# Moving Y's evictions between the statistics, and X's border issues from SP to ACT, in a two-block convolution stack

## The reference

```python
x = x + _L0_conv_ref(_gn(x), w1, w3, w5, alpha)
x = x + _L1_conv_ref(_gn(x), w, b)
```

## Time and profile before

| what | us |
|---|---|
| median of three runs | 420.05 |
| lowest and highest run | 417.27, 420.19 |
| the profiled execution | 415.32 |
| its span on the core | 413.5 |
| busy in it: PE, DVE, ACT, POOL | 318.6, 318.4, 304.0, 261.8 |

### The profile page before, as it was taken

The page is one execution under the profiler, slowest core; times in us unless marked ns, Lnnn a source line. Parts: engine busy times, 40 slices in busy tenths (PEclk is TensorE's granted clock), DMA queues, the critical chain, the costliest instruction groups (busy, mean ns, idle before and its releaser), DMA issues.

```text
span 413.5 us, 12579 instructions
## 1 busy us (share of the span) xinstructions
PE 318.6 (77%) x5206; PEld 281.8 (68%) x5206; DVE 318.4 (77%) x688; ACT 304.0 (74%) x372; POOL 261.8 (63%) x206
## 2 busy tenths in 40 slices
PE   2494849727979797979797879879897979897530
PEld 2363637616969797967696769777896779796320
DVE  7776989854778989877888696969797777599520
ACT  1317734199969999979797996989796989957320
POOL 6414525077867888768778585868585878855511
PEclk9997797995989999989898998999898999999675
DMA  7569496201996669666976789767976527701955
GB/s 154 156 193 243 122 239 140 74 6 51 201 214 182 190 186 220 169 181 195 228 192 173 197 211 220 196 192 178 219 181 191 161 61 198 201 20 48 272 165 152
DMA packets 113213, 70.01 MB, mean 169 GB/s; under 512 B 4732, under 2 KB 110084, under 8 KB 113156
## 3 DMA queue, kind: packets, MB, share of 16 engines
q1 hardware_dynamic: 106464, 65.90, 62.7%
q10 hardware_dynamic: 6692, 3.30, 3.2%
HBM read 41.10 MB, written 28.09 MB: 167 GB/s over the span
## 4 chain that ended last, share of the span: by engine, by line
DVE 46%; PE 18%; SPq 12%; DMA 10%; ACT 4%; issue 4%; ACTq 2%; POOLq 0%; POOL 0%; DVEq 0%
DVE xt L698 25%; PE ps L378 17%; DVE stats L642 17%; DMA haloX<-edge_scratch 3%; DMA xt<-in_x_dram 3%; SPq L264 3%; SPq L238 3%; ACT gn_f L552 2%; SPq L304 1%; DMA edge_scratch<-gnY 1%; ACTq L245 1%; SPq L245 1%; DMA edge_scratch<-gnX 1%; SPq L251 1%; ACT cross L562 1%
## 5 line engine op out<-in xcount | busy, mean ns | idle before, releaser
L378 PE MATMUL ps<-gnX,band 64*64 64x512 f16 x2880 | 192.4, 414 | 44.4 <-DVE xt L698 32.6
L378 PEld LDWEIGHTS ps<-gnX,band 64*64 64x64 f16 x2880 | 168.5, 189 | 61.4 <-issue 54.4
L698 DVE SCALAR_TENSOR_TENSOR xt<-ps,unscale,xt 128x512 f32<-128x512 f32 (+1 forms) x194 | 143.6, 747 | 40.1 <-PE ps L378 37.7
L868 POOL TENSOR_TENSOR gnX<-gn_f,gnX 128x768 f16<-128x768 f32 x60 | 92.7, 1544 | 53.2 <-ACT gnX L553 53.2
L552 ACT ACTIVATE gn_f<-xt,g_add,g_mul 128x768 f32<-128x768 f32 x120 | 122.1, 1017 | 5.0 <-DVE g_add L682 4.3
L642 DVE BATCH_NORM_STATS2 stats<-xt 128x6 f32<-128x384 f32 x256 | 121.1, 545 | 4.4 <-DMA xt<-in_x_dram 3.8
L378 PE MATMUL ps<-gnY,band 64*64 64x512 f16 x1728 | 107.5, 386 | 6.7 <-DVE xt L698 6.7
L868 POOL TENSOR_TENSOR gnY<-gn_f,gnY 128x768 f16<-128x768 f32 x60 | 92.6, 1544 | 30.9 <-ACT gnY L553 30.9
L378 PEld LDWEIGHTS ps<-gnY,band 64*64 64x64 f16 x1728 | 95.7, 187 | 13.9 <-issue 8.1
L877 POOL TENSOR_TENSOR xt<-xt,cross 128x512 f32<-128x512 f32 x47 | 61.5, 1311 | 47.9 <-ACT cross L562 47.8
L562 ACT ACTIVATE cross<-ps,unscale 64x512 f32<-64x512 f32 x94 | 64.1, 682 | 20.9 <-PE ps L378 19.1
(11 more groups left out here) (78 smaller groups left out, 100.3 us busy)
## 6 DMA issues: line engine op xcount, KB each, us to landing
out_dram<-xt SPq DMA_DIRECT2D x56, 384.0 KB, 4.8
xt<-in_x_dram SPq DMA_DIRECT2D x48, 384.0 KB, 6.2
band<-diag_scratch SPq DMA_DIRECT2D x48, 160.0 KB, 2.9
haloX<-edge_scratch SPq DMA_DIRECT2D x32, 185.2 KB
xt<-in_x_dram SPq DMA_DIRECT2D x20, 192.0 KB, 4.5
xt<-in_x_dram ACTq DMA_DIRECT2D x12, 192.0 KB, 4.2
out_dram<-xt SPq DMA_DIRECT2D x12, 192.0 KB, 3.4
haloY<-edge_scratch SPq DMA_DIRECT2D x30, 55.5 KB
```

The lines of the kernel that those rows point to most:

```text
L378: mm = nc.tensor.matmul(ps[to, c, half, :], weights(rows, half), moving(rows, half), start=first, stop=last)
L698: ev = nc.vector.scalar_tensor_tensor(out=here, in0=ps[frm, c, half, :].rearrange("h (b w) -> h b w", b=NB), scalar=unscale[rows, at:at + ...
L868: nc.gpsimd.tensor_tensor(gn_lo[s][:, i % 2, :, b, :, PAD:PAD + W].rearrange("p e c w -> p c e w"), gn_f[:, f_slot(s, i, b), :, :, :], gn_ ...
```

## The change

- DVE: Y's channel 0 is evicted before Y's statistics and channel 1 between batches 1 and 2 of them, in the same period; channel 1 no longer stands at the head of the next period (but for the first and the last ones).
- PE: the mean product moves behind 12 of the 15 band products of X's channel 0, the variance product behind seven of channel 1.
- ACT: in the periods that normalize an X, cross 0 comes after one batch of Y and cross 1 after two; then ACT issues X's border rows in; then follow batches 2 and 3 of Y.
- SP: one batch instead of two stands ahead of X's border rows out, and three behind; X's border rows in are issued by SP in the first two periods only.

POOL's list stays as it is.

```diff
@@ SP
-                in_and_out(j, (0, 1))
+                in_and_out(j, (0,))
                 if j + 1 < NU:
                     edges_out(sp, X, j + 1)
-                in_and_out(j, (2,))
-                if j + 1 < NU:
+                in_and_out(j, (1, 2))
+                if j < LAG:
                     edges_in(sp, X, j + 1)
                 in_and_out(j, (3,))
@@ PE
-                    conv(X, i, 0, None, i + 2 if i > 2 else None)
-                    conv(X, i, 1)
+                    conv(X, i, 0, None, i + 2 if i > 2 else None, 12, None)
+                    conv(X, i, 1, None, i + 2 if i > 2 else None, None, 7)
@@ ACT
                     normalize(X, j + 1)
-                    normalize(Y, j - 1, (0, 1, 2))
+                    normalize(Y, j - 1, (0,))
                     cross_over(y, 0)
-                    normalize(Y, j - 1, (3,))
+                    normalize(Y, j - 1, (1,))
                     cross_over(y, 1)
+                    edges_in(act, X, j + 1)
+                    normalize(Y, j - 1, (2, 3))
@@ DVE
-            def y_stats(i):
+            def y_stats(i, batches=range(NB)):
                 dve.wait_ge(evac_done[X], CG * (i + 1))
-                for b in range(NB):
+                for b in batches:
                     st = stats_of(Y, i, b)
-                st.then_inc(stats_done, 1)
+                if b == NB - 1:
+                    st.then_inc(stats_done, 1)
...
                 y = i - LAG
-                evacuate(Y, y - 1, 1)
+                if i == LAG + 1 or i > NU:
+                    evacuate(Y, y - 1, 1)
...
-                    y_stats(i)
                 evacuate(Y, y, 0)
+                if i < NU:
+                    y_stats(i, (0, 1))
+                    evacuate(Y, y, 1)
+                    y_stats(i, (2, 3))
```

## The result

The changed kernel takes 433.62 us, the median of four runs (428.57 to 435.08); the kernel before, on the same chip, 418.66 (416.60 to 420.19). The ratio is 1.032, with a 95% interval from 1.021 to 1.043: slower, by 15.0 us between the medians. The forecast was 436.0. The profiled execution took 433.9 us with a span of 432.1; before, the span was 413.5.

A forecast was written before the change was run, and what follows sets the result against it. No engine stood out as bound; ACT's list of 19.50 us was nearest. With issues 1.72, 0.08 and POOL 1.28 a load period is 22.58; with smaller terms +18.4 gives 433.7, or 438.5 from the median; forecast 436, range 426 to 447.

The forecast's parts named there:

- The sum: Whole execution: load periods of 22.58 us, 0.6 more in store periods; +18.4 on the profiled 415.3 us.
- the signs that were to show it right: Roots 22 to 23 us apart, no ACT idle before them, third X tile waiting about 1.3 for POOL, among others.
- POOL behind ACT: POOL's unedited order keeps ACT's third X tile waiting for its gn_f slot, 1.28 us in each period.
- POOL gives way: Rival: POOL doesn't hold ACT; periods of 21.3 us, about 423 on the runs' median, no change; chance 0.14.
- ACT's two issues: Issuing the two DMAs into haloX keeps ACT from all other work, 1.72 us a period in 13 periods.
- The faster rival: DMA issues run beside ACT's work; periods of 20.8 or 20.1 us, some 404 to 413; chance 0.12.
- The landing that stops ACT: ACT's issue waits for X's border rows in DRAM: 0.6 us per store period; as rival about 456, chance 0.15.
- PE and DVE ... are hidden below it, and so is what the late haloX cost PE: PE and DVE need 19.1 to 21.5 us, under the 22.58 period; late haloX costs PE 4.5 in all, also hidden.
- the queue is emptier there now: Reason for taking 0.6 us, from 0.6 to 5.1, as ACT's store-period wait for X's border rows to land.
- Alone these edits would bring the mean period from 21.46 to about 20: The DVE and PE edits by themselves gain about PE's 2.28 us wait; their loop taken as 20 us.
- What it may add is a wait for the variance: DVE's list: 2.4 us between mean and variance product, filled wholly or in part; loop 19.1 to 21.5 us.

The follow-up runs named there:

- the thin ones: Kernels with all stores, and loads from pair 4 on, cut to one channel of six: before 401.33 us, changed 416.07, changed with POOL's list reordered 403.14.
- experiment 7: Changed kernel with POOL's list reordered, plus SP with two batches ahead of X's border rows out: 454.63 us; or instead a load at SP's list head: 443.67 us.
- experiment 3: The kernel before with only the edits on ACT and SP, DVE and PE as before: 430.04 us, ratio 1.022.
- experiment 5: Changed kernel with POOL's list in ACT's order, haloX issued by SP and SP's order as before: 428.88 us, ratio 1.030.
- experiment 2: The kernel before with only the edits on DVE and PE; ACT, SP and POOL as before: 443.18 us, ratio 1.054.
- experiment 9: Changed kernel, big transfers cut to one channel of six, POOL's list in ACT's order: 403.14 us; with haloX issued by SP as well: 398.48 us.
- experiment 4: Changed kernel, but SP holds the three batches behind X's border rows until haloX has landed: 481.77 us, ratio 1.147.
- experiment 6: Changed kernel with POOL's list in ACT's order and haloX on SP, one batch ahead of X's border rows, one between them and haloX: 425.93 us, ratio 1.020.

## Why the prediction was right, point by point

*The sum.* +17.1 us was forecast for the twelve periods and 17.93 measured; 18.4 for the whole execution, and the span grew by 18.6. But two terms were mis-sized, in opposite directions. Of the signs that were to show it right, all came but the spacing of the roots, 21.1 to 21.9 and 23.2 to 25.8 us in place of 22 to 23; and one of the signs of being wrong came too, ACTIVATEs that go on during the issues.

*POOL behind ACT: right.* 1.28 us a period forecast, 1.08 in the timeline, at the tile and for the order named. Its rival (POOL gives way) falls: mending only the order gave 7.9 us between the medians of the full kernels and 12.9 of the thin ones.

*ACT's two issues: mechanism half right, size wrong.* "So ACT does nothing else meanwhile" failed. An issue started while ACTIVATEs ahead of it in the program were still running or to come (186.92 against 186.98). What cost time is the part of its 1.6 us or so that stuck out behind them: 0.36 to 1.17 us in load periods, nothing in three of the store periods. Over the twelve periods that is 7.9 us, where 12 times 1.72 = 20.6 were forecast. The earlier trace rows could not show that, since no ACTIVATE was queued ahead of the issues there. So a load period is 19.50 + 0.78 + 1.08 = 21.4 and not 22.58; measured, 21.51. The faster rival was right on half of the mechanism, and was outweighed by POOL and by haloX.

*The landing that stops ACT: absent here.* The forecast took the near end, 0.6 us in store periods. In the periods shown ACT loses nothing to it: in the store period its issues run ahead of its ACTIVATEs. The rival's waits "in the middle of the bounds", 3.5 and 0.5 us, aren't the middles: those of 0.6 to 5.1 and 0 to 2.1 are 2.85 and 1.05, though the total hardly differs (23.4 in place of 24). One more batch ahead of the border rows does stop ACT, 46.1 us in all with the issues (experiment 7).

*"PE and DVE ... are hidden below it, and so is what the late haloX cost PE": wrong.* This is the step that failed. The two DMAs were counted as issues on ACT and X's border rows as a landing; the way back, from DRAM into haloX, was taken as no slower than before. It takes 10.0 us beside six loads, PE's wait grows from 4.5 us to 30.0, and the store period to 24.93 instead of 23.18. The 4.5 us were also carried over as if PE asked for haloX when it did before, while the edits let it ask 4.55 us earlier against the root. The earlier asking weighs at least as much as the slow landing: ACT's issues with PE as before leave 7.9 us of waits (experiment 3), and the earlier PE finds haloX late on SP's queue too, 32.9 us (experiment 5). The words "the queue is emptier there now" looked at the border rows going out only; for those coming in, the batches that no longer stand ahead stand beside.

*The two errors against each other:* six load periods 1.07 shorter than forecast, five store periods 1.75 longer, period 14 shorter by 1.51: -6.4 + 8.75 - 1.5 = about +0.8, which is 17.93 against 17.1. The closeness of the total is in part luck.

*"Alone these edits would bring the mean period from 21.46 to about 20": wrong twice.* Alone they make 23.6, by the loop over ACT's cross 0 (experiment 2). With all that they need the loop of PE and DVE is 20.15, just the "I take 20" of the prediction, but only with thin transfers. And the kernel before has 20.1 then, too: its mean period falls from 21.46 to 20.41 by thinner transfers alone, 1.05 of the 1.38 us between its mean and its good period. That was not the wait of PE for DVE that the earlier trace rows lists, on which the edit bears. "What it may add is a wait for the variance" was right, and this wait took back what the edit gave (experiment 9).

What stays open: how the full transfers cost the kernel before more than the waits for them that its trace names; and whether some order of SP's list has everything in time for a PE that starts earlier. Four other orders were tried with all transfers, beside the hold of experiment 4 and the changed kernel's own, and each had some transfer late.

## What to carry to other kernels

When an engine's list is reordered, walk every list that trades buffers with it in the same order: one POOL list left as it was cost half of this loss. Before paying to shorten a loop, find what the mean period has over the good one; here most of it went away with the bytes of the transfers, which an experiment that left them out showed. And look for the wait that takes the place of the one removed: here the variance's came where PE's had been. A small DMA that somebody waits for is in time ahead of large ones in their own queue (3.0 us of waits in experiment 6), at the price of what then comes later; moved to another engine's queue it no longer waits behind them, but shares the DMA engines with all that are under way.

## What the hardware showed that was not expected

A DMA issue on ACT can start before ACTIVATEs that precede it in the program: at 186.92 it ran ahead of two of them, and cost ACT nothing; where fewer were left ahead, it held ACT for what was left of 1.6 us (1.12 at 164.21). The same two DMAs of 185 KB each took 2.7 us to land after the issue with the other queue held, 5.7 us beside six stores of 384 KB, and 10.0 us beside six loads of that size. After an idle time of 6.46 us of PE the granted clock was 0.50 from 174.10 to 177.00, and 60 matmuls took 5.11 us in place of 3.56.
